# A mixture of eight experts on 2048 tokens: sorting tokens on the chip and computing only the two chosen experts of each

## The chip, the cores and the metric

The kernel runs on one core of one Trainium2 chip. The metric is the device time of one execution in microseconds (us), as the median of several runs. A core has TensorE (PE; its weight loads are PEld), VectorE (DVE), ScalarE (ACT) and GpSimd (POOL), which compute, and SyncE (SP), which here only issues transfers. Each runs its own stream of instructions, and they meet through semaphores.

## The reference, cut to what matters

Four layers, each an attention block and a mixture of experts, act on x of 4 batches x 512 tokens x 128 features in fp32. The mixture of the first layer is the only part that the change touches:

```
x = x + L0_ffn(layernorm(x))
scores = xf @ Wg                              # 2048 x 8
w, idx = top_k(scores, 2);  w = softmax(w)
xhat = (xf - mu) * rsqrt(var + 1e-6)
normed = xhat * gamma[e] + beta[e]            # for each expert e of 8
h = relu(normed @ W1[e] + b1[e])              # 128 -> 512
out = h @ W2[e] + b2[e] + xf                  # 512 -> 128
y = sum over e of cw[:, e] * out              # cw is zero but for the two chosen experts
```

## The kernel before, in words

The residual lies in SBUF as 16 tiles of 128 tokens x 128 features (`c.resid`). Eight stages follow each other, each a block of five instruction streams with a barrier at its end (line 76). Stage 2 is `dense_experts` with the tag L0f, called in `program`. The stages hand over in two ways: the norm of the next stage is begun in the tail of this one (`nxt.norm`, lines 244 to 300), and the next stage's weights are fetched early by SyncE (`nxt.fetch.sync`, line 214).

In the L0f stage every expert is computed for every token. A step is one expert and one batch of 512 tokens, 32 steps in all. The token features lie transposed (features on partitions), so a step is 4 hidden products of 128x128 weights with 128x512 activations, and 4 result products. To reach fp32 precision in the fp32r format, every operand is split in a high and a low part, and each product is three matmuls (`split_product`, lines 95 to 97). The splits of the weights are made by GpSimd (lines 1114 to 1125), those of the hidden layer by ScalarE (line 1274) and VectorE (line 1318). The order is written out by hand: TensorE computes the hidden part of step s+2 between the results of step s. ScalarE applies the relu (line 1263). VectorE multiplies the result by each token's weight for the expert, spread over all partitions by a round trip through DRAM (lines 1090, 1091, 1361), and sums (line 1367). At the end the sums are turned back and added to the residual (lines 1202, 1372). The expert's gain is folded into its weights, its shift into its bias (line 1161).

Routing runs at the stage's start: TensorE makes the scores (line 881), VectorE scales them (892), finds the largest two of each token (806, 809), takes the softmax (849 to 855) and marks the places (821). The tokens' own part is added by `add_own` (908, 909). SyncE loads each expert's two weight arrays two experts ahead (1079, 1080).

Of the later stages only two places matter here: the third mixture loads weights with an address computed in a register (line 2222), and the second layer's attention uses plain fp32 matmuls on 128 columns (line 1688).

## Time and profile before

| | us |
|---|---|
| median of 3 runs | 1894.45 (1892.15 to 1897.48) |
| the profiled execution | 1893.99 |
| its span, first to last instruction | 1892.1 |
| mean granted TensorE clock | 0.971 of 2.4 GHz |

The profile gives, for each engine, busy time, and groups of instructions by line of the kernel. In a row, `out<-in` names what is written and read, then come shape and count; behind the bar stand busy time in us, the mean duration of one in ns, and how long the engine was idle just before them and what ended that. Matmuls overlap, so the busy time of a group over its count says how far apart they are, and the mean duration is longer than that. A plain fp32 matmul leaves two records, a transpose or an fp32r matmul one. The letters SPq and POOLq mean the sequencer of that engine.

### The profile page before, as it was taken

The page shows a single profiled execution, that of the slowest core. Times are in us where ns is not written, and L with a number is a line of the kernel's source. Part 1 is how long each engine was busy: PE and PEld are TensorE (multiplying, and loading weights), DVE is VectorE, ACT ScalarE, POOL GpSimd, SP SyncE. Part 2 cuts the span into 40 slices and gives each one's busy share as a digit, 9 for nine tenths or more (in the row PEclk, how much of TensorE's full clock was granted, in tenths as well). Part 3 has the DMA queues.
Part 4 walks back from the last instruction along what each step waited for, and adds up shares of the span by engine and source line. Part 5 has one row for each costly group of instructions (what it writes and reads, how often), then busy time and mean ns, then how long its engine had stood idle before and what let it go on. Part 6 is the DMA issues. An engine that isn't in the chain of part 4 may idle for free. (4 is left out here: it accounts for less than half of the span.)

```text
span 1892.1 us, 29275 instructions
## 1 busy us (share of the span) xinstructions
PE 1763.9 (93%) x10777; PEld 1301.5 (69%) x10777; DVE 1460.7 (77%) x2712; ACT 1036.0 (55%) x1570; POOL 708.5 (37%) x571
## 2 busy tenths in 40 slices
PE   5998999679999999999989999799899999989897
PEld 4777888555555555555557777677668899957685
DVE  6977996767777777777667888798799945668798
ACT  3656888557777777777554555355200310055685
POOL 3642321146555555655530443464112211012221
PEclk9998999889999999999988999899899999999899
DMA  2001111100000000000001221000000010000032
GB/s 68 2 15 58 67 67 56 53 1 1 1 1 1 1 1 1 1 1 1 2 19 58 67 67 56 13 2 2 23 17 22 28 56 1 0 13 1 30 120 93
DMA packets 21192, 51.48 MB, mean 27 GB/s; under 512 B 3563, under 2 KB 11383, under 8 KB 18116
## 3 DMA queue, kind: packets, MB, share of 16 engines
q1 hardware_dynamic: 20596, 49.53, 7.7%
q8 instruction: 81, 1.33, 0.3%
q14 instruction: 51, 0.42, 0.1%
q10 hardware_dynamic: 464, 0.20, 0.1%
HBM read 48.48 MB, written 1.25 MB: 26 GB/s over the span
## 5 line engine op out<-in xcount | busy, mean ns | idle before, releaser
L1618 POOL TENSOR_TENSOR sb_L_total<-sb_L_total,sb_L_probT 128x512 f32<-128x512 f32 x128 | 161.3, 1292 | 170.7 <-ACT sb_L_probT L1956 170.7
L441 POOL TENSOR_TENSOR sb_L_prob<-sb_L_prob,sb_L_rsum 128x616 f32<-128x616 f32 (+1 forms) x96 | 105.6, 1121 | 228.0 <-DVE sb_L_rsum L746 228.0
L2024 DVE TENSOR_REDUCE sb_L_tops<-banks 128x2 f32<-128x1024 f32 x128 | 156.4, 1223 | 23.7 <-PE banks L1732 22.5
L1956 ACT ACTIVATE sb_L_probT<-banks 128x1024 f32<-128x1024 f32 x128 | 124.8, 1024 | 74.7 <-PE banks L1766 74.1
L1779 PE MATMUL banks<-sb_L_probT,sb_L_v 128*64 128x512 f32 x512 | 129.0, 605 | 0.0
L2406 DVE SCALAR_TENSOR_TENSOR sb_L2f_hid<-banks,sb_L2f_weight,sb_L2f_hid 128x512 f32<-128x512 f32 x176 | 122.0, 744 | 3.0 <-PE banks L97 1.6
L1615 POOL TENSOR_TENSOR sb_L_total<-sb_L_probT 128x512 f32<-128x512 f32 x64 | 93.6, 1484 | 79.1 <-ACT sb_L_probT L1956 79.1
L2476 DVE SCALAR_TENSOR_TENSOR sb_resid<-banks,sb_L2f_weight,sb_resid 128x128 f32<-128x128 f32 x192 | 67.1, 350 | 62.3 <-PE banks L97 57.7
L1318 DVE TENSOR_TENSOR sb_L0f_hid_low<-sb_L0f_raw,sb_L0f_hid_high 128x1024 fp32r<-128x1024 f32 x64 | 88.6, 1402 | 29.1 <-ACT sb_L0f_hid_high L1274 28.5
L1255 ACT ACTIVATE sb_L1f_gate<-banks 112x512 f32<-112x512 f32 x96 | 57.5, 599 | 91.6 <-PE banks L97 91.4
L1263 ACT ACTIVATE sb_L0f_raw<-banks,sb_L0f_b 128x512 f32<-128x512 f32 x128 | 86.5, 680 | 26.7 <-PE banks L97 26.5
L529 PE MATMUL banks<-sb_ident,sb_L_prob 128*77 128x128 f32 x640 | 96.0, 283 | 5.2 <-POOL sb_L_prob L441 4.8
L263 ACT ACTIVATE sb_norm_root<-sb_norm_square 128x8 f32<-128x8 f32 (+4 forms) x16 | 3.3, 209 | 173.4 <-DVE sb_norm_square L257 149.4
L643 ACT ACTIVATE sb_L_probT<-banks 77x512 f32<-77x512 f32 x160 | 86.9, 584 | 16.9 <-PE banks L529 16.5
L1311 DVE TENSOR_TENSOR sb_L1f_raw<-sb_L1f_gate,banks 112x512 f32<-112x512 f32 x96 | 65.7, 686 | 36.6 <-PE banks L97 33.4
L529 PEld LDWEIGHTS banks<-sb_ident,sb_L_prob 128*77 128x77 f32 x640 | 70.7, 147 | 33.0 <-issue 21.1
L95 PE MATMUL banks<-sb_L2f_w_high,sb_L2f_hidT_low 128*128 128x384 f32 x256 | 86.2, 337 | 1.7 <-DVEq L2468 1.7
L96 PE MATMUL banks<-sb_L2f_w_low,sb_L2f_hidT_high 128*128 128x384 f32 x256 | 86.1, 336 | 0.0
L97 PE MATMUL banks<-sb_L2f_w_high,sb_L2f_hidT_high 128*128 128x384 f32 x256 | 86.0, 336 | 0.0
L95 PE MATMUL banks<-sb_L2f_w_high,sb_norm_low 128*128 128x512 f32 x192 | 80.7, 420 | 4.2 <-DVE sb_L2f_hid L2406 4.0
L1318 DVE TENSOR_TENSOR sb_L1f_hid_low<-sb_L1f_raw,sb_L1f_hid_high 112x512 fp32r<-112x512 f32 x96 | 84.2, 877 | 0.1
L95 PE MATMUL banks<-sb_norm_high,sb_L1f_w_low 128*112 128x512 f32 x192 | 77.8, 405 | 3.7 <-DVE sb_L1f_raw L1311 3.7
(433 smaller groups left out, 5331.2 us busy)
## 6 DMA issues: line engine op xcount, KB each, us to landing
sb_L0f_wide<-spread_L0f SPq DMA_DIRECT2D x7, 1024.0 KB, 6.3
sb_L1f_wide<-spread_L1f SPq DMA_DIRECT2D x7, 1024.0 KB, 7.1
sb_L3f_wide<-spread_L3f SPq DMA_DIRECT2D x7, 1024.0 KB, 4.9
sb_fetched<-L2f_w SPq DMA_DIRECT2D x12, 256.0 KB, 2.6
sb_fetched<-L1f_gu SPq DMA_DIRECT2D x8, 336.0 KB, 3.1
sb_fetched<-L0f_w SPq DMA_DIRECT2D x8, 259.0 KB, 2.8
sb_fetched<-L0f_w SPq DMA_DIRECT2D x8, 256.0 KB, 3.6
sb_normT<-L2f_w SPq DMA_DIRECT2D x2, 768.0 KB, 4.2
```

Source lines behind the costliest of these rows:

```text
L95: pe.matmul(out, sl, mh, start=start, stop=False)
L441: pool.tensor_tensor(grid, grid, bcast(rsum[:, n % PROBS, half], [None, KEYS]), ALU.mult).then_inc(normed, 1)
L529: last = pe.transpose(ps[0:KEYS, TURN + g % 2, a * P:(a + 1) * P], prob[:, n % PROBS, h * KEYS:(h + 1) * KEYS], c.ident[:])
L643: act.activation(probT[:, g * GROUP:(g + 1) * GROUP, :].rearrange("k h t -> k (h t)"), ps[0:KEYS, TURN + g % 2, :], ACT.Copy).then_inc(tur ...
L1263: act.activation(raw[:, s % lag, f, :], ps[:, n % HBANKS, :], func, bias=bias).then_inc(hid_read, 1)
L1318: dve.tensor_tensor(hid_low[:, s % SLOTS, at, :], raw[:, s % lag, at, :], hid_high[:, s % SLOTS, at, :], ALU.subtract).then_inc(hid_ready, 1)
L1615: pool.tensor_tensor(sums, probT[:, 0, h], probT[:, 1, h], ALU.add).then_inc(added[h], 1)
L1618: pool.tensor_tensor(sums, sums, probT[:, k, h], ALU.add).then_inc(added[h], 1)
L1779: last = pe.matmul(O[HEAD[h]], v[:, turn % 2, k, HEAD[h]], probT[:, k, h, :], start=(k == 0), stop=False)
L1956: act.activation(probT[:, k], ps[:, slot:slot + 2, :], ACT.Exp).then_inc(exped, 1)
L2024: dve.tensor_reduce(tops[:, :, k, 0], ps[:, banks:banks + 2, :], AX.X, ALU.max).then_inc(bound_read, 1)
L2406: ins = dve.scalar_tensor_tensor(out=hid[:, n, :], in0=ps[:, n % BANKS, :], scalar=share, in1=hid[:, n, :], op0=ALU.mult, op1=ALU.add)
```

## The change

The mixture of layer 0 no longer computes all experts for all tokens. `sparse_experts` takes the place of `dense_experts` for that stage. Each of the 2048 tokens is copied twice, with its weight and its own number beside the 128 features (a row of 130 words), into a table in DRAM, at a slot computed on the chip: the tokens of one expert stand together and each expert begins at a multiple of 128. VectorE and TensorE compute the slots by counting (a prefix sum over tiles and a triangular matmul over partitions). GpSimd writes the rows with 32 indirect transfers. The table has 39 blocks of 128 slots, a number fixed in advance that holds for any routing; SyncE has zeroed it during the first attention.

Then a loop of 39 blocks runs: SyncE loads a block's rows, and that block's expert's weights (both layers in one array), whose number it reads from SBUF into a register; TensorE turns the rows, ScalarE scales them by the gain, TensorE makes four hidden products in plain fp32 on 128 columns, ScalarE the relu, TensorE four result products; VectorE adds the bias, TensorE turns the result back, VectorE multiplies by the weight, and GpSimd writes the 128 rows to a results table, at the token's number, with one indirect transfer. At the end SyncE loads the results back in token order, two rows for a token, and VectorE adds them. Four row buffers, three weight buffers and two of each bank pair are in turn. The stage also drops the fetch of dense weights in the stage before it, the splits into high and low parts, and the spread of weights through DRAM.

```diff
@@ constants @@
             pool.engine_nop().then_inc(ident_ready, 1)
             made.gpsimd(pool)
+            slots.gpsimd(pool)
...
@@ Norm @@
     def normalise(self, dve, b):
-        if b >= HALVES:
+        if b >= HALVES and self.rows is None:
         for t in range(TPB):
             n = b * TPB + t
-            ins = dve.tensor_scalar(self.stage[:, b % HALVES, t, :], self.c.resid[:, n, :], self.mean[:, n:n + 1],
+            ins = dve.tensor_scalar(self.staged_tile(b, t), self.c.resid[:, n, :], self.mean[:, n:n + 1],
                                     self.inverse[:, self.kinds - 1, n:n + 1], ALU.subtract, ALU.mult)
         ins.then_inc(self.staged, 1)
+
+    def staged_tile(self, b, t):
+        return self.stage[:, b % HALVES, t, :] if self.rows is None else self.rows.staged(b)[:, t, :]
...
@@ cross_attention, sync @@
                 nxt.fetch.sync(sp)
+                if slots is not None:
+                    slots.sync(sp)
...
+SLOT = P
+BLOCKS = (2 * BATCH * SEQ + 8 * (SLOT - 1)) // SLOT
+WIDE = P + 2
+SPARE, TOKENS = BLOCKS * SLOT, BATCH * SEQ
+class Slots:
+    def __init__(self, c, ctx, fetch):
+        nc = c.nc
+        self.rows = fetch.tile["rows"]
+        self.zero = c.sb(ctx, "L0f_zero", [P, WIDE])
+        self.blocks = nc.dram_tensor("L0f_blocks", (BLOCKS * SLOT, WIDE), F32).ap()
+        self.results = nc.dram_tensor("L0f_results", (SPARE + 2 * TOKENS, P), F32).ap()
+        self.cleared = c.sem("L0f_cleared")
+    def staged(self, b):
+        return self.rows[:, b * TPB:(b + 1) * TPB, 0:P]
+    def gpsimd(self, pool):
+        pool.memset(self.zero[:], 0.0)
+    def sync(self, sp):
+        sp.dma_start(self.blocks.rearrange("(n p) w -> p n w", p=P), bcast(self.zero[:], [BLOCKS, None])).then_inc(self.cleared, 16)
...
+def sparse_experts(c, norm, fetch, nxt, slots):
+    E, F, BUFS, WBUFS, TALL = 8, 4, 4, 3, BATCH * SEQ // SLOT
+    XBANKS, HBANKS, YBANKS, BACKS = (0, 1), (2, 3), (4, 5), (6, 7)
...
+            @block.sync
+            def _(sp):
+                def load_both(j):
+                    if j >= WBUFS:
+                        sp.wait_ge(out_done, j - WBUFS + 1)
+                    e = sp.value_load(expert_no[0:1, j:j + 1], min_val=0, max_val=E - 1)
+                    sp.dma_start(both[:, j % WBUFS], c.dram["L0f_both"][bass.ds(e, 1)].rearrange("e p w -> p (e w)")).then_inc(both_in[j % WBUFS], 16)
+                sp.dma_start(w1[:], c.dram["L0f_both"][:, :, 0:W1].rearrange("e p w -> p e w")).then_inc(w_in, 16)
+                nxt.fetch.sync(sp)
+                sp.wait_ge(tabled, 1)
+                for j in range(WBUFS):
+                    load_both(j)
+                sp.wait_ge(dealt, 16 * 2 * TILES)
+                for j in range(BLOCKS):
+                    if j >= BUFS:
+                        sp.wait_ge(x_turned, j - BUFS + 1)
+                        sp.wait_ge(noted, j - BUFS + 1)
+                    sp.dma_start(got[:, j % BUFS], slots.blocks[j * SLOT:(j + 1) * SLOT]).then_inc(got_in[j % BUFS], 16)
+                    if j >= BUFS and j - BUFS + WBUFS < BLOCKS:
+                        load_both(j - BUFS + WBUFS)
+                for j in range(BLOCKS - BUFS + WBUFS, BLOCKS):
+                    load_both(j)
+                for i in range(BUFS):
+                    sp.wait_ge(sent[i], 16 * len(range(i, BLOCKS, BUFS)))
+                for b in range(BATCH):
+                    for k in range(2):
+                        at = SPARE + k * TOKENS + b * SEQ
+                        sp.dma_start(returned[:, k, b * TPB:(b + 1) * TPB], slots.results[at:at + SEQ].rearrange("(t p) d -> p t d", p=P)).then_inc(back_in[b], 16)
+            @block.gpsimd
...
+                pool.wait_ge(slots.cleared, 16)
+                pool.wait_ge(copied, 1)
+                pool.wait_ge(placed, 1)
+                for n in range(TILES):
+                    for k in range(2):
+                        pool.indirect_dma_start(out=slots.blocks, out_offset=bass.IndirectOffsetOnAxis(ap=slot_no[:, n, k:k + 1], axis=0),
+                                                in_=(slots.rows, later_rows)[k][:, n, :], in_offset=None).then_inc(dealt, 16)
+                for j in range(BLOCKS):
+                    pool.wait_ge(out_ready, j + 1)
+                    pool.indirect_dma_start(out=slots.results, out_offset=bass.IndirectOffsetOnAxis(ap=dest[:, j:j + 1], axis=0),
+                                            in_=out[:, j % BUFS, :], in_offset=None).then_inc(sent[j % BUFS], 16)
+            @block.tensor
...
+                pe.wait_ge(w_in, 16)
+                for e in range(E):
+                    for f in range(F):
+                        last = pe.matmul(ps[:, SHIFTS, f * E + e:f * E + e + 1], w1[:, e, f * P:(f + 1) * P], w1[:, e, SHIFT:SHIFT + 1], start=True, stop=True)
+                last.then_inc(shift_done, 1)
+                pe.wait_ge(numbered, 2)
+                pe.wait_ge(counts_ready, 1)
+                pe.matmul(ps[:, RANKS, 0:P], before[:], counted.rearrange("p n e -> p (n e)"), start=True, stop=False)
+                pe.matmul(ps[:, RANKS, 0:P], ones[:], counts[:, 1, E - 1:E - 1 + TILES].rearrange("p n e -> p (n e)"), start=False, stop=True)
+                pe.matmul(ps[:, RANKS, P:P + E], ones[:], counts[:, 1, E - 1 + TILES, :], start=True, stop=True).then_inc(ranked, 1)
+                def turn_rows(j):
+                    pe.wait_ge(got_in[j % BUFS], 16 * (j // BUFS + 1))
+                    if j >= 2:
+                        pe.wait_ge(x_ready, j - 1)
+                    pe.transpose(ps[:, XBANKS[j % 2], 0:SLOT], got[:, j % BUFS, 0:P], c.ident[:]).then_inc(x_turned, 1)
+                def hidden(j):
+                    pe.wait_ge(x_ready, j + 1)
+                    pe.wait_ge(both_in[j % WBUFS], 16 * (j // WBUFS + 1))
+                    if j >= 2:
+                        pe.wait_ge(hid_ready, (j - 1) * F)
+                    for f in range(F):
+                        pe.matmul(ps[:, HBANKS[j % 2], f * SLOT:(f + 1) * SLOT], both[:, j % WBUFS, f * P:(f + 1) * P], x[:, j % 2, :],
+                                  start=True, stop=True).then_inc(hid_done, 1)
+                def result(j):
+                    if j >= 2:
+                        pe.wait_ge(y_ready, j - 1)
+                    for f in range(F):
+                        pe.wait_ge(hid_ready, j * F + f + 1)
+                        last = pe.matmul(ps[:, YBANKS[j % 2], 0:SLOT], both[:, j % WBUFS, W1 + f * P:W1 + (f + 1) * P], hid[:, j % 2, f, :],
+                                         start=(f == 0), stop=(f == F - 1))
+                    last.then_inc(out_done, 1)
+                def turn_result(j):
+                    pe.wait_ge(y_ready, j + 1)
+                    if j >= 2:
+                        pe.wait_ge(out_ready, j - 1)
+                    pe.transpose(ps[:, BACKS[j % 2], 0:P], y[:, j % 2, :], c.ident[:]).then_inc(back, 1)
+                turn_rows(0)
+                turn_rows(1)
+                hidden(0)
+                for j in range(BLOCKS):
+                    if j + 2 < BLOCKS:
+                        turn_rows(j + 2)
+                    if j + 1 < BLOCKS:
+                        hidden(j + 1)
+                    result(j)
+                    if j > 0:
+                        turn_result(j - 1)
+                turn_result(BLOCKS - 1)
+                nxt.norm.turn(pe, 0, 0)
+                nxt.norm.turn(pe, 1, 1)
+            @block.scalar
...
+                def take_rows(j):
+                    act.wait_ge(x_turned, j + 1)
+                    if j >= 2:
+                        act.wait_ge(hid_done, (j - 1) * F)
+                    act.activation(x[:, j % 2, :], ps[:, XBANKS[j % 2], 0:SLOT], ACT.Copy, scale=fact[:, j, F + 1:F + 2]).then_inc(x_ready, 1)
+                def activate(j):
+                    if j >= 2:
+                        act.wait_ge(out_done, j - 1)
+                    act.wait_ge(hid_done, (j + 1) * F)
+                    for f in range(F):
+                        act.activation(hid[:, j % 2, f, :], ps[:, HBANKS[j % 2], f * SLOT:(f + 1) * SLOT], ACT.Relu, bias=fact[:, j, f:f + 1]).then_inc(hid_ready, 1)
+                act.wait_ge(tabled, 2)
+                take_rows(0)
+                take_rows(1)
+                activate(0)
+                for j in range(BLOCKS):
+                    if j + 2 < BLOCKS:
+                        take_rows(j + 2)
+                    if j + 1 < BLOCKS:
+                        activate(j + 1)
+            @block.vector
...
+                top.mark(dve, step)
+                step(dve.tensor_reduce(counted, top.hit[:], AX.X, ALU.add))
+                for gap, old, new in ((1, 2, 0), (2, 0, 1), (4, 1, 0), (8, 0, 1)):
+                    step(dve.tensor_tensor(counts[:, new, E:], counts[:, old, E:], counts[:, old, E - gap:E - gap + TILES], ALU.add))
+                dve.engine_nop().then_inc(counts_ready, 1)
...
+                dve.wait_ge(ranked, 1)
+                step(dve.tensor_tensor(filled[:], bcast(ps[:, RANKS, P:P + E], [None, TALL]), bcast(limit[:], [E, None]), ALU.is_gt))
+                step(dve.tensor_reduce(blocks_of[:], filled[:], AX.X, ALU.add))
+                step(dve.tensor_tensor(shifted[:], lower[:], bcast(blocks_of[:], [E, None]), ALU.mult))
+                step(dve.tensor_reduce(begin[:], shifted[:], AX.X, ALU.add))
+                step(dve.scalar_tensor_tensor(out=spot[:], in0=bcast(begin[:], [TILES, None]), scalar=float(SLOT),
+                                              in1=ps[:, RANKS, 0:P].rearrange("p (n e) -> p n e", n=TILES), op0=ALU.mult, op1=ALU.add))
+                step(dve.tensor_tensor(chosen[:], top.hit[:].rearrange("p n e k -> p n k e"), bcast(spot[:], [None, 2, None]), ALU.mult))
+                step(dve.tensor_reduce(slot[:], chosen[:], AX.X, ALU.add))
+                dve.tensor_copy(slot_no[:], slot[:]).then_inc(placed, 1)
+                step(dve.tensor_tensor(end[:], begin[:], blocks_of[:], ALU.add))
+                step(dve.tensor_tensor(mine[:], bcast(end[:], [BLOCKS, None]), bcast(block_no, [None, E]), ALU.is_le))
+                step(dve.tensor_reduce(expert[:], mine[:], AX.X, ALU.add))
+                step(dve.tensor_scalar(expert[:], expert[:], float(E - 1), None, ALU.min))
+                dve.tensor_copy(expert_no[:], expert[:]).then_inc(tabled, 1)
...
+                step(dve.tensor_tensor(facts_all[:], bcast(mine[:], [None, FACTS, None]), bcast(facts[:], [BLOCKS, None, None]), ALU.mult))
+                dve.tensor_reduce(fact[:], facts_all[:], AX.X, ALU.add).then_inc(tabled, 1)
...
+                def note(j):
+                    dve.wait_ge(got_in[j % BUFS], 16 * (j // BUFS + 1))
+                    dve.tensor_copy(share[:, j:j + 1], got[:, j % BUFS, P:P + 1])
+                    dve.tensor_tensor(dest[:, j:j + 1], got[:, j % BUFS, P + 1:P + 2], spare[:, j:j + 1], ALU.max).then_inc(noted, 1)
+                def add_bias(j):
+                    dve.wait_ge(out_done, j + 1)
+                    if j >= 2:
+                        dve.wait_ge(back, j - 1)
+                    dve.tensor_scalar(y[:, j % 2, :], ps[:, YBANKS[j % 2], 0:SLOT], fact[:, j, F:F + 1], None, ALU.add).then_inc(y_ready, 1)
+                def weigh(j):
+                    dve.wait_ge(back, j + 1)
+                    if j >= BUFS:
+                        dve.wait_ge(sent[j % BUFS], 16 * (j // BUFS))
+                    dve.tensor_scalar(out[:, j % BUFS], ps[:, BACKS[j % 2], 0:P], share[:, j:j + 1], None, ALU.mult).then_inc(out_ready, 1)
+                dve.wait_ge(tabled, 2)
+                note(0)
+                for j in range(BLOCKS):
+                    if j + 1 < BLOCKS:
+                        note(j + 1)
+                    add_bias(j)
+                    if j > 0:
+                        dve.wait_ge(noted, j)
+                        weigh(j - 1)
+                dve.wait_ge(noted, BLOCKS)
+                weigh(BLOCKS - 1)
+                def finish(b):
+                    dve.wait_ge(back_in[b], 32)
+                    at = slice(b * TPB, (b + 1) * TPB)
+                    step(dve.tensor_tensor(c.resid[:, at], c.resid[:, at], returned[:, 0, at], ALU.add))
+                    dve.tensor_tensor(c.resid[:, at], c.resid[:, at], returned[:, 1, at], ALU.add).then_inc(added, 1)
+                finish(0)
+                finish(1)
+                dve.wait_ge(added, 2)
+                nxt.norm.moments(dve, 0, 2)
...
-            lambda *stage: cross_attention(c, *stage, "L0", 16, 8, 8 ** -0.5, None),
-            lambda *stage: dense_experts(c, *stage, "L0f", TopTwo, "relu", P, 4, 2),
+            lambda *stage: cross_attention(c, *stage, "L0", 16, 8, 8 ** -0.5, None, slots),
+            lambda *stage: sparse_experts(c, *stage, slots),
...
-        "L0f_wg": a["L0_ffn_Wg"], "L0f_w1": packed(a["L0_ffn_W1"], a["L0_ffn_b1"], a["L0_ffn_gamma"], a["L0_ffn_beta"]), "L0f_b2": a["L0_ffn_b2"].T,
-        "L0f_w2": a["L0_ffn_W2"].reshape(E, 4, P, P).transpose(0, 2, 1, 3),
+        "L0f_wg": a["L0_ffn_Wg"], "L0f_b2": a["L0_ffn_b2"].T,
+        "L0f_both": np.concatenate([packed(a["L0_ffn_W1"], a["L0_ffn_b1"], a["L0_ffn_gamma"], a["L0_ffn_beta"]),
+                                    a["L0_ffn_W2"].reshape(E, 4, P, P).transpose(0, 2, 1, 3).reshape(E, P, 4 * P)], 2),
```

## Rows read from the trace of the kernel before

**Rows 1.** The page: busy us of each engine; DMA busy tenths, 40 slices.
```profile
PE 1763.9 (93%) x10777; PEld 1301.5 (69%) x10777; DVE 1460.7 (77%) x2712; ACT 1036.0 (55%) x1570; POOL 708.5 (37%) x571
...
DMA  2001111100000000000001221000000010000032
```
**Rows 2.** Windows: the stage's start, middle, end; busy us (count), clock, DMA share, GB/s.
```profile
137.50:163.50 26.00, 20.19 (x113) 17.41 (x114) 25.28 (x86) 12.59 (x17) 14.30 (x10) 0.81 0.09 26
163.50:341.90 178.40, 177.82 (x798) 144.43 (x797) 146.85 (x174) 141.78 (x183) 42.59 (x30) 1.00 0.18 66
341.90:352.20 10.30, 3.75 (x21) 2.47 (x19) 7.93 (x32) 1.77 (x3) 0.07 (x2) 0.81 0.00 0
```
**Rows 3.** Groups of the stage 137.5 to 352.2, by shape; first and last of six.
```profile
L95 PE MATMUL banks<-sb_norm_high,sb_L0f_w_low 128*128 128x512 f32 x128 | 52.0, 406 | 4.2 <-DVE sb_norm_low L300 4.2
...
L97 PE MATMUL banks<-sb_L0f_hid_high,sb_L0f_w_high 128*128 128x512 f32 x128 | 50.7, 396 | 0.0
```
**Rows 4.** Timeline: start us, us, engine line; two matmuls that follow each other.
```profile
329.66 0.40 PE L95 MATMUL banks<-sb_norm_high,sb_L0f_w_low 128*128 128x512 f32 x1
329.89 0.40 PE L96 MATMUL banks<-sb_norm_low,sb_L0f_w_high 128*128 128x512 f32 x1
```
**Rows 5.** Waits of the stage: who waited for whom, us in total, times, longest.
```profile
PE banks L95 <- DVE sb_norm_low L300: 4.2, 2, 3.8
```
**Rows 6.** Groups by shape, whole span: fp32 matmuls and copies of 128 columns.
```profile
L1688 PE MATMUL banks<-sb_fetched,sb_normT 128*128 128x128 f32 x256 | 33.8, 275 | 0.0
...
L1202 PE MATMUL banks<-sb_ident,sb_L0f_summed 128*128 128x128 f32 x16 | 3.0, 316 | 1.4 <-DVE sb_L0f_summed L1367 1.3
...
L647 ACT ACTIVATE sb_L_mixedT<-banks 128x128 f32<-128x128 f32 x32 | 8.9, 277 | 30.2 <-PE banks L540 30.2
...
L1161 PE MATMUL banks<-sb_fetched 128*128 128x1 f32 x64 | 7.6, 239 | 0.0
```
**Rows 7.** DMA issues: count, KB of one, median us from issue to landing.
```profile
sb_fetched<-L2f_w SPq DMA_DIRECT2D x12, 256.0 KB, 2.6
...
sb_fetched<-L0f_w SPq DMA_DIRECT2D x8, 256.0 KB, 3.6
...
sb_resid<-x SPq DMA_DIRECT2D x1, 1024.0 KB, 5.9
...
sb_fetched<-L_w SPq DMA_DIRECT2D x1, 512.0 KB, 4.1
...
spread_L0f<-sb_L0f_weightT SPq DMA_DIRECT2D x1, 64.0 KB, 2.1
```
**Rows 8.** Line 2222, SyncE's sequencer: durations ns min/median/max, first and last start.
```profile
L2222 SPq DMA_DIRECT2D sb_fetched<-L2f_w x10: 328/333/348, 1369.2 to 1479.4; - x10
L2222 SPq FUSED_REGOPS  x8: 43/46/51, 1369.0 to 1457.1; - x8
```
**Rows 9.** Timeline of the stage's start: normalising, scores, routing.
```profile
140.24 0.86 DVE L244 BATCH_NORM_STATS2 sb_norm_stats<-sb_resid 128x6 f32<-128x128 f32 x4
...
145.09 2.14 DVE L277 TENSOR_SCALAR sb_norm_stage<-sb_resid,sb_norm_mean,sb_norm_inverse 128x128 f32<-128x128 f32 x8
...
151.25 4.53 PE L881 MATMUL banks<-sb_fetched,sb_normT 128*128 128x8 f32 x32
...
159.42 0.28 DVE L892 TENSOR_TENSOR sb_L0f_rows<-banks,sb_norm_std 128x128 f32<-128x128 f32 x1
...
163.54 0.19 DVE L849 TENSOR_TENSOR sb_L0f_exps<-sb_L0f_top 128x32 f32<-128x32 f32 x1
...
164.76 0.42 DVE L821 TENSOR_TENSOR sb_L0f_hit<-sb_count,sb_L0f_placef 128x256 f32<-128x256 f32 x1
```
**Rows 10.** Two lines' durations ns min/median/max: GpSimd line 427, VectorE line 908.
```profile
L427 POOL TENSOR_TENSOR sb_resid<-sb_resid,sb_rows x4: 2352/2356/2375, 30.1 to 1256.9; 128x1024 f32<-128x1024 f32 x4
...
L908 DVE TENSOR_SCALAR sb_L0f_own<-sb_resid,sb_norm_mean,sb_L0f_total x16: 338/343/1324, 182.6 to 270.5; 128x128 f32<-128x128 f32 x16
```
**Rows 11.** Window of 4 us in the stage's start, columns as in rows 2.
```profile
154.00:158.00 4.00, 1.77 (x9) 1.68 (x8) 4.00 (x3) 1.85 (x2) 3.92 (x3) 0.50 0.00 0
```

124 lines of the change are left out of this document (115 added, 9 removed).

## The prediction

> **What bounds the kernel now.** I read the engines' totals first: TensorE is busy 93% of the span, so a stage that computes less on it can shorten the kernel, if nothing else takes its place [rows 1]. Then the stretches of the one stage that changes, from the first mixture's start (137.5 us) to the first work of the next stage (352.2 us), 214.7 us in all. In its long middle, 178.4 us, TensorE is busy 177.8 us at clock 1.00, while VectorE (146.9) and ScalarE (141.8) have slack; both ends, 26.0 and 10.3 us, are chains at clock 0.81 [rows 2]. The groups of that stretch show what fills it: six groups of 128 matmuls of 512 columns. They are 8 experts x 4 batches x 4 parts x 2 layers x 3 products of high and low parts = 768, one every 0.23 us (329.66 and 329.89 in the timeline), 179 us in all [rows 3, 4]. The view of waits agrees: the longest that TensorE's matmuls have in the stage is 4.2 us in total, for the normalised rows near its start [rows 5]. So the stage is bound by TensorE's columns, and everything outside 137.5 to 352.2 is left alone.
>
> **What the change removes.** All 768 products, with the splitting on GpSimd, VectorE and ScalarE that fed them. In their place stand 39 blocks (39 = (2 x 2048 + 8 x 127) / 128 rounded down) of 128 rows: 4992 row passes where 16384 stood. They are plain fp32 matmuls, which leave two records each. Rows of the same shape, 128x128 against 128 columns, show 256 records in 33.8 us, 0.132 us each; the transposes show 3.0 us for 16, 0.19 each [rows 6]. A block is 8 matmuls (16 x 0.132 = 2.11 us) and 2 transposes (0.38): 2.49 us, and 39 of them 97 us. If TensorE still bound the stage, it would save 80 us less the new prologue and tail. I do not think it does. ScalarE has 5 copies a block of 128x128 out of PSUM at 0.28 us, 1.4 us [rows 6]; VectorE has two such and two of one column, about 1.0 us. Both hide under TensorE, with a microsecond to spare.
>
> **The loop: the weights' ring.** Each block loads its expert's whole weights, 128 x 1030 x 4 bytes = 527 KB, through a ring of three buffers. SyncE waits for out_done(j), reads the expert's number into a register, issues the load for block j+3; hidden(j+3) waits for it, and result(j+2) stands behind hidden(j+3) in TensorE's order. So from out_done(j) to out_done(j+2), two periods, there pass: the load's latency L, then the 4 hidden and 4 result matmuls, 2.11 us. Period T = (L + 2.11 + 0.05) / 2, whenever that is over 2.49.
> L is made of four parts. The last matmul ends 0.15 us after the next could start (0.28 long, 0.13 apart), and a semaphore hop takes 0.1 by the gaps of the timelines. The transfer: 512 KB landed in 4.1 us behind another, a 256 KB one of the third mixture in 2.6, and of the pair that makes up one expert's weights today the second, 256 KB issued 0.4 us behind the first, in 3.6 [rows 7]. The bounds are 3.3 and 4.5; I take 3.9, as row loads and result scatters run beside it. The address from a register costs nothing to speak of: the third mixture does it with a 46 ns register operation and a 333 ns issue [rows 8]. The read of the register from SBUF has no row. Below, it is no more than such a register operation, 0.05; above, it is a small transfer's round trip, 2.1 us for 64 KB [rows 7]. I take 0.8, nearer the register side since one word is read. L = 0.15 + 0.1 + 0.8 + 3.9 = 4.95, T = 3.55 us (bounds 2.9 and 4.5); TensorE would be busy 70% of it. 38 periods are 134.9 us. The row loads in the same SyncE queue are issued ahead of that wait for rows needed two blocks later, so they add 0.4 us of issue and no wait. Nothing else queues behind it there until the loop ends.
> The Trainium skill ("DMA: Bandwidth & Descriptors", Latency and other measured facts) gives such a read a floor of about 0.6 us; by it alone T would be 3.45, and the kernel 4 us shorter than my sum.
>
> **The prologue, 25 us to the known slots.** VectorE need not split the first batch: moments start 2.7 us earlier than in the trace, and the normalised rows end at 145.0 instead of 147.2. Turns and two copies: 146.9. Scores: 32 records, 4.5 us, 151.4 [rows 9]. From the scores' copy to the softmax's shift VectorE took 4.3 us (159.4 to 163.7), then come mark (0.43), a sum, four shifted adds at 0.28 with a hop: 158.0 [rows 9]. TensorE has the 32 shift columns in between, 64 records at 0.119 us, 7.6, to 159.0; the ranks are out by 160.0 [rows 6]. Eight dependent VectorE steps of 64 to 256 columns, 0.2 to 0.43 each, end at 162.7. The block tables (two steps of 1872 columns, some 2 us each) and the 32 own-row steps, which were in the old stage too, lie under the next part.
>
> **The deal, 32 scatters in a row.** GpSimd issues 32 indirect transfers of 128 rows of 520 bytes, and no block may start before all have landed: this is wholly on the path. No row shows one. Below, SyncE's issue of a transfer, 0.33 us [rows 8]; above, GpSimd's own pass over 128x1024, 2.36 us [rows 10]. I take the middle, 1.35: it must build 128 rows' addresses, more than one issue and less than a thousand columns. 43.2 us (bounds 10.6 and 75.5). Then landing 2.2, the first row load 2.2, and turn, copy, hidden, activate, result of block 0: 4. Together 51.6 us.
> By the Trainium skill (the same page and section) a transfer from GpSimd costs about 1 us to emit; the deal would be 32 us and the kernel 1900.
>
> **The tail, 20.5 us.** After the last out_done: bias, turn, weight 0.95; the last scatter 1.35 + 2.2; the return loads 3; the residual adds of batches 0 and 1, 4 x 0.7. Then what the trace shows from the first statistics (341.90) to the next stage's first work (352.2): 10.3 [rows 2]. In the old stage the last TensorE work lay beside this chain; now nothing does. Zeroing the blocks (2.6 MB) is issued by SyncE in the first attention, over 100 us before its use, where the DMA engines' busy digit is 0 [rows 1]: nothing. The 2.1 MB of biases and first weights is issued at the stage's start and wanted 14 us later; at 5.9 us for 1024 KB, as the first load of the residual, it lands about 149 [rows 7]: nothing, and 2 us if it doesn't.
>
> **Sum.** 25 + 51.6 + 134.9 + 20.5 = 232.0 us against 214.7: 17.3 slower. The profiled execution took 1893.99 (span 1892.1, 1.9 around it), 0.5 under the median of 1894.45. 1893.99 + 17.3 = 1911.3; I say 1911.
>
> **Rivals.**
> 1. The ring is quicker than I price it (the other side: faster). It decides at T = 3.55 - 17.3 / 38 = 3.09 us, L = 4.0. For it: 256 KB landed in 2.6 us, and a read at its lower bound. L = 0.15 + 0.1 + 0.1 + 3.3 gives T = 2.9: 1911 - 25 = 1886; at TensorE's own 2.49 it is 1871. A deal at 0.8 us a scatter does the same (-18). Against it: 512 KB rows show 4.1. Chance 0.26.
> 2. Scatters are dear. VectorE works on the own rows during the deal, and the trace has the two engines holding each other up: the same 128x128 step took 0.34 us as a rule and 1.32 beside GpSimd's work [rows 10]. At 2.36 us a scatter: 1911 + 32 = 1943; over 3.55 the sends would set the period too. Chance 0.20. The Trainium skill ("SBUF — State Buffer", the trap in which DVE blocks DMA) says GpSimd can't write descriptors while VectorE holds the shared ports, five times the time for a transfer in its example; the row of 1.32 agrees that the two block each other.
> 3. The clock falls. TensorE waits over a microsecond in each period, and where it starved before the rows show less: 154 to 158 us, with TensorE busy 1.77 of 4, had 0.50, the lower of its two levels (1.2 GHz) [rows 11]. Then 2.11 becomes 4.2 and T 4.6: 1951. Against it: the prologue and the tail, busy 78% and 36%, had 0.81 on average [rows 2], and the loop's gaps are far shorter than theirs. Chance 0.09.
> The forecast holds the other 0.45, 1896 to 1928.
>
> **How the numbers follow.** Rival 1 is faster beyond 0.3% (5.7 us, about what a measurement of this kernel tells from none) in all but its edge: faster 0.25. Within: 0.08, its edge and the forecast's lower one. Slower: 0.67. The range leaves out a tenth on either side: 1876 (rival 1 nearly at TensorE's bound) to 1951 (rivals 2 and 3).
>
> **What would show it.** Right: 32 scatters on GpSimd of 1.0 to 1.7 us each with TensorE idle 40 to 55 us; out_done every 3.4 to 3.8 us with TensorE's longest waits on the weights' load; 43 to 48 us of stage outside loop and deal. Wrong: TensorE waiting for GpSimd or for ScalarE in the loop; a period under 3.1; a register read over 2 us; loop clock near 0.5.

## The result, and the profile after

The changed kernel took 1909.65 us (median of 4 runs, 1905.34 to 1910.78) where the kernel before took 1894.61 (4 runs): ratio 1.0079, 95% interval 1.0064 to 1.0093. Run again beside other kernels it took 1914.10 (6 runs), ratio 1.0101 (1.0083 to 1.0119). It is slower, by 15 us in the first measurement and 21 in the second.

The page of the changed kernel, engines' totals and the lines by 40 slices:

```profile
PE 1673.6 (88%) x10668; PEld 1240.0 (65%) x10668; DVE 1354.9 (71%) x2757; ACT 944.5 (50%) x1573; POOL 726.2 (38%) x610
...
PE   5984366479999999999989999899889999989898
...
PEclk9995699789999999999998999899899999999899
DMA  4012376400000000000001111000000010000032
```

TensorE is busy less, 88% of the span instead of 93% [rows 1], and the kernel is longer all the same: the fourth to the eighth digit of PE, in which this stage lies, are 4, 3, 6, 6, 4. The stage in its four parts (busy time of each engine, number of instructions, then granted clock, DMA share, GB/s): prologue, deal up to the first block's result, loop, tail.

```profile
137.15:168.88 31.73, 24.06 (x110) 23.26 (x110) 14.57 (x99) 6.00 (x7) 1.19 (x7) 0.53 0.29 88
168.88:221.50 52.62, 6.02 (x29) 5.47 (x30) 17.56 (x50) 3.20 (x11) 32.93 (x32) 0.51 0.25 77
221.50:346.10 124.60, 83.92 (x676) 76.00 (x674) 28.27 (x151) 53.68 (x186) 35.31 (x37) 1.00 0.67 191
346.10:367.64 21.54, 2.16 (x9) 1.44 (x8) 10.96 (x36) 1.77 (x3) 2.04 (x3) 0.60 0.39 107
```

The four stretches are 230.5 us against 214.7 [rows 2]: 15.8 longer, close to the 15.0 between the medians. The two profiled executions themselves differ by less, 1905.34 against 1893.99 us: behind this stage the same code took 4 us less in the changed one (experiment 11 has these times), so the stage's own end in the trace is the better measure of what the change did. TensorE's work in the loop fell from 177.8 us to 83.9, as the change intends; but the loop takes 124.6 us, and 105.9 us of prologue, deal and tail stand around it in which TensorE has 32 us of work.

**Prologue.** The timeline of the changed kernel there (start, duration, engine, line, then in brackets the idle time before and what ended it):

```profile
141.52 2.14 PE L288 MATMUL banks<-sb_ident,sb_fetched 128*128 128x128 f32 x8 [5.87 <-DVE sb_fetched L278]
...
144.34 6.99 PE L1561 MATMUL banks<-sb_fetched,sb_normT 128*128 128x8 f32 x32 [0.69 <-ACT sb_normT L295]
...
151.19 13.79 PE L1566 MATMUL banks<-sb_L0f_w 128*128 128x1 f32 x64
...
156.50 1.27 DVE L1676 TENSOR_TENSOR sb_L0f_counts<-sb_L0f_counts 128x128 f32<-128x128 f32 x4
...
164.84 0.77 PE L1570 MATMUL banks<-sb_L0f_counts,sb_L0f_before 128*128 128x128 f32 x2
...
166.31 0.29 DVE L1683 TENSOR_TENSOR sb_L0f_filled<-banks,sb_L0f_limit 128x128 f32<-128x128 f32 x1 [7.50 <-PE banks L1572]
...
169.81 1.17 POOL L1547 DMA_INDIRECT L0f_blocks<-sb_fetched,sb_L0f_slot_no  x1 [31.37 <-DVE sb_L0f_slot_no L1691]
...
171.10 2.11 DVE L1705 TENSOR_TENSOR sb_L0f_facts_all<-sb_L0f_mine,sb_L0f_facts 128x1872 f32<-128x1872 f32 x1
171.28 2.76 POOL L1547 DMA_INDIRECT L0f_blocks<-sb_L0f_later_rows,sb_L0f_slot_no  x1 [0.30 <-issue]
...
173.24 2.10 DVE L1706 TENSOR_REDUCE sb_L0f_fact<-sb_L0f_facts_all 128x234 f32<-128x1872 f32 x1
...
174.35 0.96 POOL L1547 DMA_INDIRECT L0f_blocks<-sb_fetched,sb_L0f_slot_no  x1 [0.31 <-issue]
```

TensorE idles 5.87 us, and from there on, 141.5 to 165, it has 0.50 of the clock. Its scores take 6.99 us (4.53 before, [rows 9]), its 64 records for the shift columns 13.79. The counts are ready near 157.8, but the rank products (line 1570 and the next two) stand behind the shift columns in TensorE's queue, and VectorE waits 7.50 us.

Two VectorE passes over 1872 columns lie beside the first scatters, and they don't do the same. The scatter that begins during the product of two tensors (line 1705) takes 2.76 us and ends 0.83 us after that pass; the next, which runs beside the reduction of the same columns (line 1706), takes 0.96.

**Loop.** One turn of the ring: a result's last products, SyncE's load for three blocks later, and that block's hidden products. Then the DMA view (KB each, median us from issue to landing) and the three instructions of the register read:

```profile
276.59 1.06 PE L1594 MATMUL banks<-sb_L0f_hid,sb_L0f_both 128*128 128x128 f32 x8
...
277.68 0.35 DVE L1723 TENSOR_SCALAR sb_L0f_y<-banks,sb_L0f_fact 128x128 f32<-128x128 f32 x1 [2.48 <-PE banks L1594]
...
278.40 0.35 SPq L1506 DMA_DIRECT2D sb_L0f_both<-L0f_both  x1
...
282.40 1.13 PE L1586 MATMUL banks<-sb_L0f_x,sb_L0f_both 128*128 128x128 f32 x8 [1.02 <-ACT sb_L0f_x L1632]
...
284.46 0.35 DVE L1723 TENSOR_SCALAR sb_L0f_y<-banks,sb_L0f_fact 128x128 f32<-128x128 f32 x1 [2.52 <-PE banks L1594]
```

```profile
sb_L0f_both<-L0f_both SPq DMA_DIRECT2D x39, 515.0 KB, 3.8
...
sb_L0f_got<-L0f_blocks SPq DMA_DIRECT2D x39, 65.0 KB, 3.6
...
L0f_blocks<-sb_fetched,sb_L0f_slot_no POOLq DMA_INDIRECT x16, 2.3
```

```profile
L1505 SPq TENSOR_LOAD <-sb_L0f_expert_no x39: 262/266/471, 170.4 to 337.8; - x39
L1505 SPq FUSED_REGOPS  x39: 152/152/186, 170.9 to 338.1; - x39
L1505 SPq SEQ_ASSERT  x39: 18/18/33, 171.2 to 338.3; - x39
```

The bias of a block starts as soon as its result is done: at 277.68, and two blocks later at 284.46. That is 6.78 us, and within them 0.72 to the issue, 4.0 to the hidden products, 2.06 for hidden and result. The row at 282.40 names a copy of ScalarE as the releaser, but the copy that these products read began at 277.90 and took 0.37 us, so it had ended four microseconds before: of the several semaphores waited for, the weights' came last.

From the first block's result to the last one's there are 123.8 us (221.57 to 345.38; the third stretch above ends 0.7 us later), 3.26 us a period over 38 (the expectations below have 3.28, from the 124.6). Over 33 of them, from the second block's result on, it is 3.36; both measures come back below.

### The profile page after: what moved, and what is told of

Its sections match the earlier page's. It is cut to its first block and busy times, and to the rows that moved or that the text cites. A ratio compares the mean times of both kernels' runs of the same rounds, so it can differ in the third digit from the quotient of the medians.

```text
span 1903.6 us, 29463 instructions
## 1 busy us (share of the span) xinstructions
PE 1673.6 (88%) x10668; PEld 1240.0 (65%) x10668; DVE 1354.9 (71%) x2757; ACT 944.5 (50%) x1573; POOL 726.2 (38%) x610
## 3 DMA queue, kind: packets, MB, share of 16 engines
q0 software_dynamic: 2272, 4.69, 0.7%
## 5 line engine op out<-in xcount | busy, mean ns | idle before, releaser
L535 PEld LDWEIGHTS banks<-sb_ident,sb_L_prob 128*77 128x77 f32 x640 | 70.7, 147 | 32.6 <-issue 20.5
L1723 DVE TENSOR_SCALAR sb_L0f_y<-banks,sb_L0f_fact 128x128 f32<-128x128 f32 x39 | 13.7, 350 | 101.5 <-PE banks L1594 101.5
L1586 PE MATMUL banks<-sb_L0f_x,sb_L0f_both 128*128 128x128 f32 x312 | 45.7, 291 | 40.4 <-ACT sb_L0f_x L1632 32.3
L1639 ACT ACTIVATE sb_L0f_hid<-banks,sb_L0f_fact 128x128 f32<-128x128 f32 x156 | 44.6, 368 | 73.0 <-PE banks L1586 73.0
```

The source lines that it names most:

```text
L535: last = pe.transpose(ps[0:KEYS, TURN + g % 2, a * P:(a + 1) * P], prob[:, n % PROBS, h * KEYS:(h + 1) * KEYS], c.ident[:])
```

## The experiments

Theory: the loop is the weights' ring, and prologue and deal are in series with it. A buffer is held from a block's hidden products to its result, and as TensorE makes the next block's hidden products in between, that is one period and 2.1 us. So (number of buffers) periods are L + one period + 2.1, and the period is (L + 2.1) / (buffers - 1). Rivals: the transfers' rate binds, not their latency; the read and the scatters are hidden or cost something else; the clock.

**1. Four weight buffers.**

```
-    E, F, BUFS, WBUFS, TALL = 8, 4, 4, 3, BATCH * SEQ // SLOT
+    E, F, BUFS, WBUFS, TALL = 8, 4, 4, 4, BATCH * SEQ // SLOT
```

> Four weight buffers where three were, nothing else. Theory A, the ring of weights sets the period: with three buffers two periods hold the load's latency and 8 matmuls, T = (L + 2.16) / 2 = 3.28 us as the trace of the changed kernel shows it, L = 4.4. With four, three periods hold them, (4.4 + 2.16) / 3 = 2.2, under TensorE's own 2.49 us: T falls to 2.5 to 2.7, 38 periods give back 22 to 30 us, some 1883 us, under the kernel before. Theory B, the DMA engines set it (busy 0.70 in the loop at 198 GB/s): the latency only grows with the rate, T stays over 3.0 and the time falls by less than 10 us. Theory C, something else paces the loop (GpSimd's scatters, ScalarE): no change within 3 us.

Measured: 1882.90 us, ratio 0.9954 (0.9937 to 0.9970), faster than the kernel before. The 40 us from 260, first of the changed kernel, then with four buffers, and the latter's DMA and longest waits of TensorE from 230 to 310 (in total, times, longest):

```profile
260.00:300.00 40.00, 26.92 (x219) 24.41 (x218) 8.83 (x48) 17.03 (x60) 11.49 (x12) 1.00 0.70 198
```

```profile
260.00:300.00 40.00, 32.29 (x267) 29.21 (x265) 11.05 (x60) 22.07 (x74) 14.55 (x16) 1.00 0.87 253
```

```profile
sb_L0f_both<-L0f_both SPq DMA_DIRECT2D x39, 515.0 KB, 4.8
...
sb_L0f_got<-L0f_blocks SPq DMA_DIRECT2D x39, 65.0 KB, 4.5
```

```profile
PE banks L1578 <- DMA sb_L0f_got<-L0f_blocks: 13.6, 21, 1.4
```

One number raised by one gives 27 us in the stage (the next stage's first product is at 342.42 instead of 369.76). The period falls from 3.26 to 2.56 us (over 33 periods, from 3.36 to 2.63); the load takes 4.8 us instead of 3.8 as the DMA engines go from 0.70 to 0.87 of their time, and what ends TensorE's waits is now the rows, not the weights. Part of the timeline with four buffers:

```profile
256.74 0.35 DVE L1723 TENSOR_SCALAR sb_L0f_y<-banks,sb_L0f_fact 128x128 f32<-128x128 f32 x1 [2.40 <-PE banks L1594]
...
258.74 0.35 DVE L1723 TENSOR_SCALAR sb_L0f_y<-banks,sb_L0f_fact 128x128 f32<-128x128 f32 x1 [1.27 <-PE banks L1594]
...
259.45 0.35 SPq L1506 DMA_DIRECT2D sb_L0f_both<-L0f_both  x1
259.90 0.37 SPq L1518 DMA_DIRECT2D sb_L0f_got<-L0f_blocks  x1
...
264.77 0.33 PE L1578 MATMUL banks<-sb_ident,sb_L0f_got 128*128 128x128 f32 x1 [0.56 <-DMA sb_L0f_got<-L0f_blocks]
...
266.94 0.35 DVE L1723 TENSOR_SCALAR sb_L0f_y<-banks,sb_L0f_fact 128x128 f32<-128x128 f32 x1 [2.06 <-PE banks L1594]
```

Two things can be read here. Where nothing holds TensorE up, two results are 2.00 us apart (256.74 and 258.74), so its own work on a block is 2.0 us and not the 2.49 of the prediction and of the expectations; the loop is not at TensorE's bound. And there is a second chain in place of the weights' ring: the row load at 259.90 is issued 1.16 us after a result, as it stands in SyncE's queue behind the weights' load that waited for this result; its rows are turned 4.87 us later, and the result three blocks after the first comes 2.17 us behind that. By the medians of the trace these are 1.17, 4.69 and 2.16 us, 8.0 in three periods, 2.67 us each, where 2.63 is measured. With three weight buffers the same rows are turned 5.39 us after their issue though they land in 3.6, so they had 1.8 us to spare.

**2. Two weight buffers** (the same line with 2).

> Two weight buffers where three were. Theory A: one period then holds the load's latency and 8 matmuls, T = 4.4 + 2.1 = 6.5 us against 3.28, 38 x 3.2 = +122 us, some 2030 us. Theory B (DMA engines' throughput): they are less loaded, landing is quicker, T under 5, less than +65 us. Theory C: no change.

Measured: 2098.71 us, ratio 1.1094 (1.1071 to 1.1117). Two turns of TensorE in it:

```profile
284.49 2.04 PE L1586 MATMUL banks<-sb_L0f_x,sb_L0f_both 128*128 128x128 f32 x8 [4.12 <-issue]
286.33 1.91 PE L1594 MATMUL banks<-sb_L0f_hid,sb_L0f_both 128*128 128x128 f32 x8
...
292.96 2.05 PE L1586 MATMUL banks<-sb_L0f_x,sb_L0f_both 128*128 128x128 f32 x8 [4.29 <-issue]
```

The ring is right in direction, but the period is 8.3 us and not the 6.6 (0.7 + 3.8 + 2.1) it would be at full clock: with waits of 4.2 us the clock falls (0.60 in 240 to 280), 8 records take 2.04 us instead of 1.06, and 0.7 + 3.8 + 3.8 is 8.3. This is the prediction's rival 3, which three buffers just escape: their waits are 1 to 1.3 us and the clock is 1.00.

**3. No register read.**

```
-                    e = sp.value_load(expert_no[0:1, j:j + 1], min_val=0, max_val=E - 1)
-                    sp.dma_start(both[:, j % WBUFS], c.dram["L0f_both"][bass.ds(e, 1)]...
+                    sp.dma_start(both[:, j % WBUFS], c.dram["L0f_both"][j * E // BLOCKS])...
```

> The expert of each block's weight load is a constant of the program, so SyncE reads no register from SBUF (the blocks' weights are then not those of the routing; everything else is computed). Theory A: the read and its checks, 0.27 + 0.15 + 0.07 = 0.5 us in the trace, leave L; T falls by 0.25 us, the time by 9 us, to some 1900. Theories B and C: within 3 us of the changed kernel.

Measured: 1894.21 us, ratio 1.0013 (1.0003 to 1.0023). Its load is issued at 277.19, 280.21, 282.94; the period over 33 blocks is 2.97 us where the changed kernel has 3.36. That gives back more than 9 us: 15 by the medians, 12 by the ratios, 14 at the next stage's first product (355.69 instead of 369.76). What goes is all that lies between the wait and the issue, 0.7 us with the read, near nothing without it; half of 0.7 in each of 38 periods is 13 us.

**4. The same read twice.**

```
+                    again = sp.value_load(expert_no[0:1, j:j + 1], min_val=0, max_val=E - 1)
                     e = sp.value_load(expert_no[0:1, j:j + 1], min_val=0, max_val=E - 1)
```

> SyncE reads each block's expert number from SBUF into a register twice, one read after the other, and uses the second; nothing else differs from the changed kernel. Theory (the read is part of the ring's latency L, period = (L + 2.2) / 2): a read shows 0.27 to 0.5 us in SyncE's records, so L grows by that, the period by 0.13 to 0.25, and 38 periods by 5 to 9.5 us: 1915 to 1919, ratio 1.011 to 1.013. Rival 1 (taking the read out gave back 15 us, so a read costs 0.8 us in the ring, as the prediction had it): 15 us more, 1925, ratio 1.016. Rival 2 (the row loads and the deal hide it): ratio as the changed kernel's.

Measured: 1924.17 us, ratio 1.0157 (1.0136 to 1.0178); the unaltered changed kernel, measured beside it and told below, had 1914.10. A read more costs 10 us, just over the theory's upper end of 9.5. The two ratios are each uncertain by 0.002, so the times alone don't tell the theory from rival 1 and its 15 us. The trace does: from the start of a block's bias to the issue of the weights' load it is 1.26 us (median of the blocks) where the changed kernel has 0.71, so a read with its checks is 0.55 us, and half of that in 38 periods is 10 us. The clock takes a part too, how much wasn't separated: of four stretches of 20 us from 215, the third has 0.81 here, where the unaltered kernel has 1.00.

```profile
215.00:235.00 20.00, 13.86 (x85) 12.87 (x86) 3.16 (x19) 7.89 (x27) 2.88 (x3) 0.80 0.39 113
235.00:255.00 20.00, 13.05 (x107) 11.77 (x105) 4.51 (x24) 8.52 (x30) 5.15 (x6) 1.00 0.63 187
255.00:275.00 20.00, 14.07 (x89) 13.59 (x90) 2.96 (x16) 6.92 (x24) 4.45 (x5) 0.81 0.61 175
275.00:295.00 20.00, 12.98 (x96) 11.81 (x95) 4.43 (x24) 7.64 (x27) 5.76 (x6) 0.94 0.59 166
```

**5. The changed kernel again.**

> The changed kernel itself, unaltered, on the same chip and in the same rounds as the two that follow, to have its time beside theirs. Ratio to the kernel before as measured: 1.0079, between 1.006 and 1.0095; the profiled execution's period of the weights' ring 3.2 to 3.5 us.

Measured: 1914.10 us, 1.0101 (1.0083 to 1.0119), the period 3.41 over 33 blocks; the ratio is a little over what was expected and over its own interval of the first time. What two measurements of one kernel differ by, 4 us, bounds what the smaller comparisons here can tell.

**6. Half the weights' bytes.** From block 3 on only the first layer's 259 KB are loaded.

```
+                    some = W1 + W2 if j < WBUFS else W1
+                    sp.dma_start(both[:, j % WBUFS, 0:some], c.dram["L0f_both"][bass.ds(e, 1), :, 0:some]...
```

> From the fourth block on only the first layer's half of each block's weights is loaded (265 KB in place of 527; the result products use the ones of blocks 0 to 2). Theory A: landing falls from 3.8 to about 2.7, as 256 KB loads land in the third mixture, L = 3.3, T = 2.75; 38 x 0.53 = -20 us, some 1889. Theory B: the bytes halve, T falls to TensorE's 2.49 or near it, -28 us or more. Theory C: no change.

Measured: 1894.77 us, ratio 1.0013 (0.9997 to 1.0028). The landing falls from 3.8 to 2.8 us at a DMA share of 0.48; the period is 2.96. Half the bytes give back a quarter of the latency: 2.8 us of it is there for a half-size load as well.

**7. The shift columns behind the ranks** (the five lines of that loop moved below the three rank products).

> The 32 shift columns (64 records, 13.8 us with the clock at its lower level) are issued by TensorE behind the three rank products instead of ahead of them; nothing else differs from the changed kernel. Theory (they stood on the path to the slots): in the changed kernel VectorE waited 7.5 us for the ranks although the counts were ready 7 us before, so the first scatter comes 6 to 7 us earlier (near 163 us instead of 169.8), and the median falls by 6 us against the changed kernel, ratio to the kernel before 1.0045. Rival (the wait only moves: the facts of the blocks need the shifts, and VectorE or the deal ends no earlier): ratio stays at 1.008.

Measured: 1902.13 us, ratio 1.0045 (1.0032 to 1.0058).

```profile
159.57 6.75 PE L1571 MATMUL banks<-sb_L0f_w 128*128 128x1 f32 x31
159.76 0.29 DVE L1683 TENSOR_TENSOR sb_L0f_filled<-banks,sb_L0f_limit 128x128 f32<-128x128 f32 x1 [0.63 <-PE banks L1567]
...
163.26 1.18 POOL L1547 DMA_INDIRECT L0f_blocks<-sb_fetched,sb_L0f_slot_no  x1 [24.50 <-DVE sb_L0f_slot_no L1691]
```

VectorE's wait is 0.63 us instead of 7.50 and the first scatter 6.55 us earlier, as the theory had it. The order of two independent jobs in TensorE's queue was worth 6 us by the ratio to the first measurement, 11 by that to the second. In the profiled execution the next stage's first product is only 3.5 us earlier (366.27): the loop took 126.8 us instead of 123.8, with one period of 5.5, and nothing here tells why.

**8. The prologue kept warm** (7, and products with the identity).

```
+                keep_busy(pe, c, 4, 17)
                 norm.turn(pe, 2, 0)
                 norm.turn(pe, 3, 1)
+                keep_busy(pe, c, 4, 3)
                 norm.wait(pe)
```

> As shift_behind_ranks, and 17 fp32 products of 128x128 with the identity, into a bank that is not in use, ahead of TensorE's first turns of the stage and 3 more ahead of its scores, to fill the 5.9 us in which TensorE stood idle at clock 0.50. Theory (the slow prologue is the clock): the granted clock in 145 to 165 us is above 0.50, the scores take 4.5 us instead of 7.0, and the first scatter comes another 2 to 4 us earlier; ratio to the kernel before about 1.003. Rival (the clock is not held by so little work, or VectorE's chain of steps ends last whatever TensorE does): as shift_behind_ranks within 1 us, 1.0045, or worse by what the added products take.

Measured: 1901.75 us, ratio 1.0036 (1.0024 to 1.0049).

```profile
137.19 4.03 PE L103 MATMUL banks<-sb_ident 128*128 128x128 f32 x34 [1.55 <-PEq L76]
...
143.88 4.18 PE L1563 MATMUL banks<-sb_fetched,sb_normT 128*128 128x8 f32 x32
```

In the trace the scores take 4.18 us instead of 6.99, at a clock of 0.87 instead of 0.50, and the first scatter is at 159.65, 3.6 us before that of 7. The next stage's first product is 6.3 us earlier (360.02), of which the slow period in the loop of 7 has a part. The times don't separate the two: their intervals overlap. So the clock's part of the slow prologue is shown by the trace, and its price in the kernel's time is not.

**9. Half the deal.**

```
-                    for k in range(2):
+                    for k in range(1):
```

The wait for the deal is halved to fit, and both return loads read the first choice's half.

> Only the first choice of each token is dealt: 16 indirect transfers in place of 32. The rows of the second choices stay zero in the table and the first choice's result is read back twice, so the second expert's part is left out; the loop still runs 39 blocks. Theory (every scatter is on the path, at 1.26 us apiece): 16 x 1.26 = 20 us less than the changed kernel, so about 1889, ratio 0.998. Rival 1 (the deal waits for DMA landings, or the weights' loads or block tables end last): under 8 us less, ratio 1.004 or more. Rival 2 (later scatters are dearer than early ones, as VectorE's own-row steps run beside them): savings other than 20, the spacing of the 16 then not 1.26.

Measured: 1890.15 us, ratio 0.9976 (0.9967 to 0.9986). Against the changed kernel's two ratios that is 19.5 and 23.7 us less for 16 scatters, 1.2 to 1.5 us apiece; in the traces the loop's first new load moves from 222.29 to 201.22. Every scatter is on the path. The profiled execution, the slowest of the ten, lost 6 us of that again in its loop: after one wait of 3.13 us at 281.4 TensorE made 8 records in 2.05 us, half its usual rate, and the next stage's first product is at 355.25, 14.5 us earlier than in the changed kernel.

**10. Four buffers and the warm prologue together.**

> All three parts together: four weight buffers in place of three, the shift columns behind the ranks, and the filling products. Theory (the parts lie one after the other on the path and add up): 1883 of the four-buffer kernel less what warm_prologue gains on the changed kernel (8 to 10 us): 1874, ratio to the kernel before 0.990. Rival (with four buffers the loop is bound by TensorE and the transfers, whatever the prologue does, but the prologue's gain is still in front of it): no rival mechanism would take it away except that all four weight loads are issued under the deal; then 1880 or more, ratio 0.9935.

Measured: 1869.25 us (6 runs), ratio 0.9879 (0.9860 to 0.9898): faster than both kernels, 25 us less than the one before and 40 to 45 less than the changed one. The parts add up, and a little more: 1874 was expected, whose ratio of 0.990 is at the interval's edge.

**11. A fifth buffer.**

> As four_buffers_warm with five weight buffers. With four, period (4.8 landing + 0.65 + 2.2) / 3 = 2.55 us and 2.63 to 2.69 were measured, TensorE's own work 2.49. Theory A (the ring still ends last now and then): period 2.50 to 2.55, 4 to 6 us less than four_buffers_warm, 1864, ratio 0.985. Theory B (the transfers bind: 0.87 of the DMA engines' time is in use at 253 GB/s, and the row loads that TensorE now waits for come late for that): period stays 2.6 to 2.7, landing of the weights grows to 6 us or more, ratio 0.988 as four_buffers_warm.

Measured: 1876.63 us, ratio 0.9903 (0.9885 to 0.9920), so not faster than 10. The period over 33 blocks is 2.67 us against 2.69, the DMA share 0.88, and the rows end TensorE's waits as in 1: the weights' ring is no longer what ends last, and theory A is out. Theory B isn't shown by that. The chain of the row loads explains the same period: a row load stands in SyncE's queue behind a weights' load that waits for the result five blocks back, and with five weight buffers it still does, for the order of the queue follows the four row buffers. Its parts here are 1.15, 4.76 and 2.16 us, 2.69 a period. No run moves the row loads ahead of that wait, so whether their place in the queue or the rate of the transfers keeps the period at 2.7 stays open.

The 7 us by which 11 is slower than 10 are not made in this stage. The next stage's first product in the kernel before, in the changed one, in 10 and in 11 (spans 1892.1, 1903.6, 1864.0, 1876.9):

```profile
354.26 0.62 PE L95 MATMUL banks<-sb_L_cT_high,sb_L_w_low 128*128 128x308 f32 x1 [3.92 <-POOL sb_L_w_low L1596]
```

```profile
369.76 0.63 PE L95 MATMUL banks<-sb_L_cT_high,sb_L_w_low 128*128 128x308 f32 x1 [4.77 <-POOL sb_L_w_low L1939]
```

```profile
333.74 0.62 PE L95 MATMUL banks<-sb_L_cT_high,sb_L_w_low 128*128 128x308 f32 x1 [4.77 <-POOL sb_L_w_low L1941]
```

```profile
334.17 0.62 PE L95 MATMUL banks<-sb_L_cT_high,sb_L_w_low 128*128 128x308 f32 x1 [4.79 <-POOL sb_L_w_low L1941]
```

Up to there 10 and 11 are equal to 0.4 us. Behind it the same code takes 1537.8, 1533.8, 1530.3 and 1542.7 us in the four executions. What makes this part vary by 12 us wasn't tried (in the other nine runs it took 1536 to 1540); in 784 to 934 us the fourth has 0.98 of the clock and the third 1.00.

## Why the prediction was right, step by step

1911 was said and 1909.65 measured, the stage 232.0 and 230.5 us. The bound was right: the loop is the weights' ring and TensorE no longer sets it (experiments 1 to 4), and prologue, deal and tail stand in series with it (7, 9). But the sum is closer than its terms, for errors of opposite sign cancel:

- Prologue: 25 predicted, 31.7 measured. What was mis-sized is the pricing of TensorE's records (4.5 us of scores, 0.119 us a shift record) from rows at a higher clock. The changed kernel has nothing in TensorE's queue while VectorE normalises, the clock is 0.50, the scores take 7.0 us and a shift record 0.215. All but half a microsecond of the 6.7 comes through the shift columns: the steps named them as standing "in between" and held them for ready by 159.0; they ended at 165.0, 7 us behind the counts. The scores' 2.5 us cost nothing, by luck, since TensorE could begin them 2.5 us earlier than said, and the counts were ready at 157.8 where 158.0 was said. VectorE's steps from the first statistics to the normalising took 3.15 us instead of the 4.85 before. One of these steps is shown below.
- Deal and first block: 51.6 predicted, 52.6 measured. A scatter was put at 1.35 us, between 0.33 and 2.36; it is 0.96 us busy and 0.30 to the next, 1.26, and 1.32 on average with the two slow ones. So the middle of wide bounds was luck, and no run tests the reason given for it. What was gained there and at the landings went to the first block, which took 6.1 us instead of 4 at a clock of 0.55.
- Loop: 134.9 predicted, period 3.55; 123.8 measured, period 3.26. The landing was right, 3.9 and 3.8 us. Mis-sized is the time from out_done to the issue: 1.05 us predicted (0.8 of it for the read), 0.72 measured. The read with its checks is 0.55 us by experiment 4, of which the load's own record is 0.266. The Trainium skill ("DMA: Bandwidth & Descriptors", Latency and other measured facts) has about 0.6 us as the floor of such a read; the 0.55 here is near it, a little under. TensorE's own 2.49 us a block was wrong too, 2.0 in experiment 1, for its records follow each other every 0.11 us and not every 0.132 and 0.19; the forecast didn't rest on it, but rival 1's lowest time, 1871, and the lower end of the range did.
- Tail: 20.5 predicted (its terms add up to 20.6); from the last result on, 22.3 measured. The return loads landed in 4.2 us where 3 was said.

The step of VectorE's normalising, before and after; the slow one lies beside a split of the weights on GpSimd (142.53, 1.30 us), which the change drops:

```profile
142.59 1.27 DVE L252 TENSOR_SCALAR sb_norm_work<-sb_norm_work 128x4 f32<-128x4 f32 x1
```

```profile
138.63 0.16 DVE L253 TENSOR_SCALAR sb_norm_work<-sb_norm_work 128x4 f32<-128x4 f32 x1
```

Rival 1 was the nearest: the period went over half of the way from 3.55 to its deciding point of 3.09. Experiments 1, 3 and 6 cross that point (2.63, 2.97, 2.96 us over 33 blocks); the last two end level with the kernel before and not under it, since the prologue is 6.7 us longer than priced. Rival 2 happened once: beside the 2.11 us pass of line 1705 a scatter took 2.76 us. Of the thirty-one others only the first was over 1.04 us (1.17), though VectorE worked on the own rows beside them. Rival 3 happened in the prologue, where it was not looked for, in the loop of experiment 2, and for one turn in that of 9.

## What to carry to other kernels

Where a ring's slot is refilled only after its last use, as many periods as there are slots hold the latency and the time for which a slot is held. Here a slot is held for one period and 2.1 us, which gives (latency + 2.1) / (slots - 1). The latency has what the issuing queue does between its wait and its issue in it. Work this out before a kernel with less arithmetic is called faster, and try one more slot first, here one digit and 27 us. Then look for the next chain: a load that stands in a queue behind another load's wait has that wait in its own latency. When a stage's arithmetic is halved, its prologue and tail lose their cover: price them at the clock that an idle TensorE has, and put what others wait for ahead of what is wanted later in TensorE's queue. Look for terms that cancel: a sum within 2 us held errors of 7 and 11.

## What the runs showed of the hardware

- An indirect scatter of 128 rows of 520 bytes costs GpSimd 1.26 us apiece (0.96 busy, 0.30 to the next) and lands in 2.3 us.
- In each of the twelve traces of the changed kernel and its variants, just one scatter took over 1.2 us, namely 2.4 to 2.8: the one that began during VectorE's 2.11 us product of two tensors over 1872 columns. Beside the 2.10 us reduction of the same columns a scatter took 0.96.
- With nothing to wait for, records of plain fp32 products of 128x128 against 128 columns follow each other every 0.11 us at clock 1.00 (8 hidden records begin 0.89 us ahead of the result's, at 270.49 and 271.38 in the trace of experiment 1).
- A read of one word from SBUF into SyncE's register, with its checks, delayed the next issue by 0.55 us.
- A 515 KB load lands in 3.8 us at 198 GB/s and 4.8 at 253 GB/s; one of 259 KB in 2.8 us at 139 GB/s.
- TensorE waits of 1 to 1.3 us in every 3.3 left the clock at 1.00; with a half microsecond more of latency it showed 0.81 in places, after a single wait of 3.1 us 8 records took 2.05 us instead of 1.06, and with waits of 4.2 us in every 8.3 it showed 0.60.
